# Cross attention in float32r halves: the softmax normaliser moves from z to the exponentials

## The reference

```
x_q = w_qk @ y          x_k = w_qk @ x          x_v = w_v @ x + b_v
energy[n, m] = x_q[:, n] . x_k[:, m]
attention = softmax(energy, over m)
attention = attention / (1e-7 + attention.sum over n)
x_r = x_v @ attention
out = x + relu(w_t @ (x - x_r) + b_t)
```

## Time and profile before

| | us |
|---|---|
| median of 3 runs | 1972.63 (1972.2 to 1974.23) |
| span of the profiled execution | 1972.2 |
| the fastest run's own time, which agrees with that span | 1972.2 |
| PE matmul busy | 1955.4 (99%), 9304 instructions |
| DVE busy | 1649.1 (84%), 1706 instructions |
| ACT busy | 990.9 (50%), 1345 instructions |
| POOL busy | 308.2 (16%), 136 instructions |
| mean granted TensorE clock | 0.996 |

### The profile page before, as it was taken

One profiled execution on the slowest core, in us unless ns is written; L12 is line 12 of the kernel. 1 busy time (PEld: TensorE's weight loads), 2 busy tenths in 40 slices (PEclk: granted clock), 3 DMA queues, 4 the chain that ended last, 5 costly groups with the idle time before them and its releaser, 6 DMA issues.

```text
span 1972.2 us, 24915 instructions
## 1 busy us (share of the span) xinstructions
PE 1955.4 (99%) x9304; PEld 1637.3 (83%) x9304; DVE 1649.1 (84%) x1706; ACT 990.9 (50%) x1345; POOL 308.2 (16%) x136
## 2 busy tenths in 40 slices
PE   8999999999999999999999999999999999999997
PEld 7888888888888888888888888888888888888886
DVE  5888888888888888888888888888888888888887
ACT  4554545545455455455454554545545455545453
POOL 1111101111111111111111111101111111111110
PEclk9999999999999999999999999999999999999999
DMA  2011110111111111111111111111111111111101
GB/s 101 22 43 65 64 54 35 43 58 64 64 43 43 43 64 64 43 43 43 64 64 45 40 43 64 64 64 40 45 43 64 64 43 43 43 64 64 43 22 43
DMA packets 28510, 101.65 MB, mean 52 GB/s; under 512 B 3152, under 2 KB 3920, under 8 KB 28496
## 3 DMA queue, kind: packets, MB, share of 16 engines
q1 hardware_dynamic: 27952, 101.46, 14.2%
q10 hardware_dynamic: 544, 0.00, 0.0%
HBM read 67.90 MB, written 33.55 MB: 51 GB/s over the span
## 4 chain that ended last, share of the span: by engine, by line
PE 98%; DVE 1%; DMA 0%; issue 0%; ACT 0%; SPq 0%; DVEq 0%
PE slot L507 53%; PE pv L542 35%; PE slot L522 9%; DMA x_sb<-x 0%; PE slot L549 0%; DVE res L398 0%; DVE x_lo L468 0%; DVE res L403 0%; DVE s_inv_all L383 0%; DVE colsum_T L369 0%; DVE neg_max L334 0%; DVE s_part L374 0%; DVE colsum L363 0%; ACT p_hi L236 0%; ACT x_hi L212 0%
## 5 line engine op out<-in xcount | busy, mean ns | idle before, releaser
L229 ACT ACTIVATE p_sb<-slot,neg_max 128x1024 f32<-128x1024 f32 x256 | 286.1, 1118 | 805.6 <-DVE neg_max L334 805.6
L334 DVE TENSOR_REDUCE neg_max<-slot 128x1 f32<-128x1024 f32 x256 | 311.1, 1215 | 108.3 <-PE slot L507 108.3
L344 DVE TENSOR_TENSOR p_lo<-p_sb,p_hi 128x1024 fp32r<-128x1024 f32 x256 | 311.1, 1215 | 83.2 <-ACT p_hi L236 83.2
L363 DVE SCALAR_TENSOR_TENSOR colsum<-p_sb,row_inv,colsum 128x1024 f32<-128x1024 f32 x224 | 371.2, 1657 | 0.0
L507 PE MATMUL slot<-gx_hi,y_hi 128*128 128x512 f32 x1024 | 320.4, 394 | 0.0
L507 PE MATMUL slot<-gx_lo,y_hi 128*128 128x512 f32 x1024 | 316.5, 390 | 0.0
L507 PE MATMUL slot<-gx_hi,y_lo 128*128 128x512 f32 x1024 | 315.4, 389 | 0.0
L185 POOL TENSOR_TENSOR y_lo<-y_sb,y_hi 128x1024 fp32r<-128x1024 f32 x64 | 154.0, 2406 | 798.0 <-ACT y_hi L219 798.0
L179 POOL TENSOR_TENSOR x_lo<-x_sb,x_hi 128x1024 fp32r<-128x1024 f32 x63 | 152.6, 2422 | 804.1 <-ACT x_hi L212 804.1
L542 PE MATMUL pv<-p_hi,v_hi 128*128 128x512 f32 x1024 | 277.2, 392 | 0.0
L542 PE MATMUL pv<-p_hi,v_lo 128*128 128x512 f32 x1024 | 275.7, 391 | 0.0
(11 more groups left out here) (66 smaller groups left out, 2373.9 us busy)
## 6 DMA issues: line engine op xcount, KB each, us to landing
x_sb<-x SPq DMA_DIRECT2D x64, 512.0 KB, 3.7
y_sb<-y SPq DMA_DIRECT2D x32, 1024.0 KB, 4.7
out<-res SPq DMA_DIRECT2D x64, 512.0 KB, 2.9
wqk_sb<-w_qk SPq DMA_DIRECT2D x1, 256.0 KB, 3.5
wtT_sb<-w_t_T SPq DMA_DIRECT2D x1, 256.0 KB, 4.1
wv_sb<-w_v SPq DMA_DIRECT2D x1, 256.0 KB, 5.5
bv_sb<-b_v ACTq DMA_DIRECT2D x1, 1.0 KB, 3.4
bt_sb<-b_t ACTq DMA_DIRECT2D x1, 1.0 KB, 4.7
```

The lines of the kernel that those rows point to most:

```text
L229: nc.scalar.activation(p_sb[j % 2][:, :], slot[s][:, :], ACT.Exp, bias=neg_max[par][:, j:j + 1], accum_out=row_sum[par][:, j:j + 1]).then_ ...
L334: nc.vector.tensor_reduce(neg_max[par][:, j:j + 1], slot[s][:, :], AX.X, ALU.max, negate=True).then_inc(max_done, 1)
L344: nc.vector.tensor_tensor(p_lo[t][:, :], p_sb[t][:, :], p_hi[t][:, :].bitcast(FP32), ALU.subtract).then_inc(p_lo_done, 1)
L363: nc.vector.scalar_tensor_tensor(out=colsum[par][:, :], in0=p_sb[j % 2][:, :], scalar=inv, in1=colsum[par][:, :], op0=ALU.mult, op1=ALU.ad ...
```

## The change

The row sum's inverse no longer scales z, but the exponentials. `p_high` on ACT reads p_sb with scale row_inv, and so waits for the inverse instead of the exponential. `p_low` on DVE becomes a scalar_tensor_tensor, p_sb times row_inv minus p_hi. z is split once per half batch, straight from the PSUM slot: z_hi by ACT (`z_high`, in `z_copy`'s place), z_lo by a new DVE instruction of 1024 elements (`z_low`). `v_high` and `v_low`, of 256 elements and once per row tile, are gone. PE waits for z_lo where it waited for z_copied before it wrote the slot again, and `pv_tile` has one wait fewer.

```diff
-            def p_high(b, j):
-                act.wait_ge(exp_done, NT * b + j + 1)
+            def p_high(b, par, j):
+                act.wait_ge(inv_done, NT * b + j + 1)
                 if j >= 2 or not isinstance(b, int) or b > 0:
                     act.wait_ge(pv_done, NT * b + j - 1)
-                nc.scalar.activation(p_hi[j % 2][:, :], p_sb[j % 2][:, :], ACT.Copy).then_inc(p_hi_done, 1)
+                nc.scalar.activation(p_hi[j % 2][:, :], p_sb[j % 2][:, :], ACT.Copy,
+                                     scale=row_inv[par][:, j:j + 1]).then_inc(p_hi_done, 1)
-            def z_copy(b, half, s, first=False):
+            def z_high(b, half, s, first=False):
                 act.wait_ge(z_done, 2 * b + half + 1)
                 if not first:
-                    act.wait_ge(v_lo_done, NT * (b - 1) + HT * (half + 1))
-                nc.scalar.activation(z_sb[:, half * HT:(half + 1) * HT, :],
+                    act.wait_ge(pv_done, NT * (b - 1) + HT * (half + 1))
+                nc.scalar.activation(z_hi[:, half * HT:(half + 1) * HT, :],
...
-            def v_high(b, par, j):
...
# DVE
+                nc.vector.scalar_tensor_tensor(out=p_lo[t][:, :], in0=p_sb[t][:, :],
                                                scalar=row_inv[par][:, j:j + 1],
+                                               in1=p_hi[t][:, :].bitcast(FP32), op0=ALU.mult,
+                                               op1=ALU.subtract).then_inc(p_lo_done, 1)
+            def z_low(b, half, s):
+                dve.wait_ge(z_hi_done, 2 * b + half + 1)
+                rows = slice(half * HT, (half + 1) * HT)
+                nc.vector.tensor_tensor(z_lo[:, rows, :], slot[s][:, :].rearrange("p (t o) -> p t o", t=HT),
+                                        z_hi[:, rows, :].bitcast(FP32), ALU.subtract).then_inc(z_lo_done, 1)
...
# DVE, batch
                 row_inverse(b, par, 0)
                 if not first:
                     part_sum(b - 1)
-                low_parts(b, par, 0)
+                    z_low(b, 0, other)
+                p_low(b, par, 0)
...
# PE, pv_tile
+                if j % HT == 0:
+                    pe.wait_ge(z_lo_done, 2 * b + j // HT + 1)
+                passes = ((z_hi, p_hi[t], p_hi_done), (z_lo, p_hi[t], p_hi_done), (z_hi, p_lo[t], p_lo_done))
+                for n, (z, p, ready) in enumerate(passes):
+                    if n != 1:
+                        pe.wait_ge(ready, NT * b + j + 1)
...
# PE, batch, ahead of energy(b, par, 1, other); the same edit stands ahead of w_part(b - 1, 1 - par, 0, ...)
-                pe.wait_ge(z_copied, 2 * b + 1)
+                pe.wait_ge(z_lo_done, 2 * b + 1)
```

More of the change, by code:

```diff
@@ L90, in xattn_kernel @@
         y_hi, y_lo = sb("y_hi", [P, KT, N], FP32R), sb("y_lo", [P, KT, N], FP32R)
-        z_sb = sb("z_sb", [P, NT, C])
+        z_hi, z_lo = sb("z_hi", [P, NT, C], FP32R), sb("z_lo", [P, NT, C], FP32R)
         res = sb("res", [P, KT, N])
@@ L103, in xattn_kernel @@
         p_lo = [sb(f"p_lo{i}", [P, N], FP32R) for i in range(2)]
-        v_hi = [sb(f"v_hi{i}", [P, C], FP32R) for i in range(2)]
-        v_lo = [sb(f"v_lo{i}", [P, C], FP32R) for i in range(2)]
         pv = ctx.enter_context(nc.psum_tensor("pv", [P, KT, N], FP32))
@@ L267, in batch @@
                 if first:
-                    z_copy(b, 0, other, first=first)
+                    z_high(b, 0, other, first=first)
                 exponent(b, par, 0, own)
                 if not first:
-                    z_copy(b, 0, other)
-                p_high(b, 0)
-                v_high(b, par, 0)
+                    z_high(b, 0, other)
+                p_high(b, par, 0)
                 if not first:
@@ L277, in batch @@
                 exponent(b, par, 1, other)
-                p_high(b, 1)
-                z_copy(b, 1, own, first=first)
-                v_high(b, par, 1)
+                z_high(b, 1, own, first=first)
+                p_high(b, par, 1)
                 tile(b, par, 2, other)
@@ L412, in tile @@
                 row_inverse(b, par, j)
[L414 to L416 removed]
             def batch(b, par, first=False, last=False):
                 own, other = par, 1 - par
+                if first:
+                    z_low(b, 0, other)
                 row_max(b, par, 0, own)
@@ L431, in batch @@
                     scale(b - 1, 0)
-                low_parts(b, par, 1)
+                z_low(b, 1, own)
+                p_low(b, par, 1)
                 if not first:
@@ L533, in pv_tile @@
                 t = j % 2
-                passes = ((v_hi[t], p_hi[t], v_hi_done),
-                          (v_lo[t], p_hi[t], v_lo_done),
-                          (v_hi[t], p_lo[t], p_lo_done))
-                for n, (v, p, ready) in enumerate(passes):
-                    pe.wait_ge(ready, NT * b + j + 1)
+                if j % HT == 0:
[4 more added lines that the diff above has]
+                        pe.wait_ge(ready, NT * b + j + 1)
                     for mt in range(KT):
```

49 lines of the change are left out of this document (15 added, 34 removed).

## The result

| | before | after |
|---|---|---|
| median, us | 1972.41 (1972.19 to 1974.23, 4 runs) | 1994.09 (1992.26 to 1995.31, 4 runs) |
| ratio, 95% interval | | 1.0108 [1.0096, 1.012] |
| span of the profiled execution | 1972.2 | 1990.5 |

The direction was forecast, the size was not: 21.7 us instead of 7.0, and outside the range. A run's own time is its span plus 1.8 us (1992.26 belongs to the span of 1990.5), so the span 1972.2 of before belongs to an execution of about 1974, and the fastest run's 1972.2, which the table ahead of the prediction sets beside it as the same, is the time of another. Of all executions of this case one, the profiled one of e15, ran at a granted clock of 0.654 (2788.5 us), and it is left out.

What follows compares the result with a forecast made beforehand. PE, busy 1955.4 of 1972.2 us, bounds the kernel. E1's wait 7.1, E7's 0 and tail -0.15 give 7.0 us on the median 1972.6: 1979.6 us, 0.35% slower; 8-in-10 range 1974.0 to 1988.5.

Steps and rivals of the forecast that it cites:

- The question: For each edit: how late is the last thing that PE waits for, and when does PE get there.
- first rival: Both waits bite: E7's wait costs 0.1 to 0.4 us per batch on top; 1983 to 1992 us, chance 0.22.
- E1's wait: Energy step 1 of batches 1 to 31 waits for DVE's z_lo; 0.23 us per batch, 7.1 us.
- s_part: DVE result ahead of z_lo at a batch's end; 0.15 us earlier than before.
- E7's wait: Energy step 7 of batches 0 to 30 waits for gx_lo; cost taken as nothing, upper bound 9 us.
- slack: Room between gx_lo's hand-over and E7's due start; 0.3 us left of 1.9.
- T: End of POOL's x_lo, start of the chain to gx_lo; 0.3 us earlier than before, gx_lo ending at T + 10.4.
- there is nothing to win on PE but part of the tail: PE's matmuls stay the same in shape and order; only earlier issue or waits change the time.
- z_lo of the second half: PE needs it nearly 6 us behind the end of z1; hidden, no cost.
- no PV tile waits: p_hi and p_lo come some 1.3 us later near the batch's end, yet no PV tile waits; nothing.
- PE issues faster with one wait fewer: Rival: 256 removed PV waits give 0.03 us each, 7.7 us; chance 0.04 for faster issue with a gain.
- DVE's sum: DVE's busy time over the run; about 94 us less, with no effect on the span.

Runs made afterwards that it cites:

- e18: The changed kernel with z_hi, z_lo allocated behind p_lo and an unused pad at z_sb's place, both new waits kept; 1990.53 us.
- e15: The changed kernel without its two new waits, p_hi and p_lo behind z but moved by 1024 bytes; 1963.0 us at full clock.
- e11: The changed kernel without its two new waits, z_hi and z_lo behind p_lo, the copy of z at z_sb's place; 1974.55 us.
- e1: The changed kernel with PV's wait on its second pass put back; 1997.1 us.
- e3: The changed kernel with z_lo allocated last, so that z_hi alone stands at the new offset; 1995.55 us.
- e4: The changed kernel with z first copied to SBUF by ACT, E1 waiting for that copy only, z_hi and z_lo split later; 1991.44 us.
- e7: The changed kernel without its two new waits: z copied to SBUF first and split from there, gx ahead of p in tile 6; 1983.59 us.
- e10: The kernel before, no instruction changed, v_hi and v_lo allocated right behind z_sb; 1983.95 us.
- e16: The changed kernel with both new waits, p_hi and p_lo allocated right behind z_hi and z_lo; 1990.29 us.
- e12: The kernel before, no instruction changed, v and p allocated right behind z_sb, all at offset 768; 1962.05 us.

## Why the prediction was wrong

**The question was right, its answer half so.** "How late is the last thing that PE waits for" found both waits at the right two places. With PE at its old pace (e18) they cost 1990.53 - 1973.08 = 17.5 us (7.0 forecast), and 16.0 above e11, which has neither. That lies in the first rival, "both waits bite" (1983 to 1992 us, given 0.22), near its upper end; the 1994.09 of the change itself lies above it.

**E1's wait: mechanism right, 0.34 instead of 0.23 us.** At the old pace E1 starts 0.33 later (11.51 against 11.18 behind PV6) and takes 0.01 longer than before. Two terms were off. s_part came 0.04 earlier, not 0.15, most of it because p_hi, which stands in this chain, takes 1.15 and not 1.06. Behind the reciprocal of tile 7 E1 was to start after 751.36 - 742.60 = 8.76 us and started after 757.08 - 748.26 = 8.82, 0.06 later. And I let E1 take 2.80 behind a wait, from a step of batch 0, where the steps that waited here took 2.86. Both together are 0.12 us, 31 times, 3.7 us.

**E7's wait: taken as nothing, about 0.25 us at the old pace, and little in the profiled execution of after.** In e18 E7 starts 0.12 later in the mean behind E1 and takes 2.86 instead of 2.73. The steps of the chain were the right ones; two of its sizes were not, the time from T to gx_lo and T itself. T is the end of the second x_lo, below 790.94 + 2.40 = 793.34:

```profile
790.94 2.40 POOL L148 TENSOR_TENSOR x_lo<-x_sb,x_hi 128x1024 fp32r<-128x1024 f32 x1 [6.68 <-ACT x_hi L181]
796.71 2.55 POOL L154 TENSOR_TENSOR y_lo<-y_sb,y_hi 128x1024 fp32r<-128x1024 f32 x1 [3.37 <-ACT y_hi L188]
```

```profile
791.73 2.70 DVE L322 SCALAR_TENSOR_TENSOR colsum<-p_sb,row_inv,colsum 128x1024 f32<-128x1024 f32 x1
795.72 1.28 DVE L303 SCALAR_TENSOR_TENSOR p_lo<-p_sb,row_inv,p_hi 128x1024 fp32r<-128x1024 f32 x1 [1.22 <-ACT p_hi L205]
798.06 2.29 DVE L322 SCALAR_TENSOR_TENSOR colsum<-p_sb,row_inv,colsum 128x1024 f32<-128x1024 f32 x1
801.64 1.29 DVE L303 SCALAR_TENSOR_TENSOR p_lo<-p_sb,row_inv,p_hi 128x1024 fp32r<-128x1024 f32 x1 [1.22 <-ACT p_hi L205]
802.84 1.22 DVE L288 TENSOR_TENSOR gx_lo<-slot,gx_hi 128x1024 fp32r<-128x1024 f32 x1
```

```profile
794.54 1.15 ACT L205 ACTIVATE p_hi<-p_sb,row_inv 128x1024 fp32r<-128x1024 f32 x1 [1.48 <-DVE row_inv L298]
```

```profile
804.19 0.66 PE L465 MATMUL slot<-gx_hi,y_hi 128*128 128x512 f32 x2
```

The colsum ends at T + 1.09 (forecast 1.08) and p_hi starts at T + 1.20 (1.19). Then p_hi takes 0.09 longer, y_lo runs 2.55 instead of 2.41 beside the p_lo at 795.72, the second colsum ends at T + 7.01 (6.8), p_hi is 0.09 longer again, p_lo starts at T + 8.30 (8.0), and gx_lo ends at T + 10.72 (10.4); the median over the run is 10.73. That 0.3 alone is nearly the whole slack.

T was to come 0.3 earlier than before. Counted from the start of E1 it was at 36.34 us before (medians), was forecast at 787.1 - 751.08 = 36.02, and came at 36.24 in after and 36.19 in e18: only 0.10 to 0.15 earlier. The first x_lo, held up by p_lo, ended later than forecast, and finish ended with it, 28.27 us behind E1 (28.40 before; 28.02 forecast); in e18 the second x_lo also started later behind finish, 5.65 us for 5.53 before. Together gx_lo came 0.5 us later than forecast in e18, at 46.91 behind E1 for 46.42, and the slack is gone. In after E7 starts here 0.13 behind gx_lo, on the edge, so that 0.1 us in the load of x decides from batch to batch; e1, e3 and e4, other executions of nearly the same kernel, waited 11 to 13 us in all.

The prices that were missing were of single instructions: p_hi twice, y_lo, and the first x_lo. For y_lo the prediction had the Trainium skill's rule beside it (SBUF — State Buffer, section "SBUF: two separate sides") and took 0.15 from it as a delay of no weight; the row shows 0.14, and p_hi took another 0.18. The first x_lo stands behind a p_lo in the same way and is longer by 0.18, but there the prediction had no such delay.

**The steps that failed** are two that were put at nothing. The first is the cost of E7's wait ("I take the cost as nothing"). At the old pace it is about 0.25 us per batch, 31 times, 7.8 us; with the 3.7 of E1 this makes 7.0 into 18.5, where e18 measured 17.5, and it is what carries the time past the range's 1988.5. The second is the sentence "The change issues the same matmuls, with the same shapes and in the same order, so there is nothing to win on PE but part of the tail", which took PE's pace as fixed. The same matmuls read their weights from another place. Alone that costs 31 x (61.09 - 60.79) = 9.3 us of period, 9.0 to 10.5 us in time (e7 against e11, e10 against before). In the changed kernel it costs only 1994.09 - 1990.53 = 3.6 us, since a slower PE waits less: 17.5 + 3.6 = 21.1 of the 21.7. That it is no plain sum, as I still expected before e16 (7.7 + 4.5 + 10), is what e16 and e18 showed: the sum comes near 21.7 by luck, but it gave e16 1975.6 us, and e16 took 1990.29.

**The rest.** z_lo of the second half is hidden, as forecast, and no PV tile waits. "PE issues faster with one wait fewer" is refuted by e1. DVE's sum fell by 23 us rather than 94, since `finish` took over the hold-up by POOL with 64; neither sum mattered. The tail's 0.15 can't be seen.

## What to carry to other kernels

When an engine that is never idle gets a wait, ask whether the awaited result hangs on that engine's own last step: such a chain closes into a loop with a period of its own, and then what PE gains elsewhere comes back as waiting. A slack of 0.3 us in a ten-step chain needs the price of each instruction in its new form and among its new neighbours (here the Copy with a scale from a tensor, and POOL's x_lo and y_lo beside p_lo). And a change of allocations is a change of PE's pace: when tensors come or go, compare matmul starts, and try the layout by itself, which here was worth more (0.6% gained, e12) than the loss that was forecast for the change (0.35%).
